# Three PSUM banks for attention scores and two for projections, instead of two and three, in a fused attention and feed-forward kernel

## The chip, the cores and the metric

The kernel runs on one core of one Trainium2 chip. The metric is device time in microseconds, the median of three runs. The kernel before took 746.64 us (746.29 to 746.75).

## What is computed

A transformer block on x of shape (4, 512, 512): layer norm, then attention with 16 heads of 32 and a linear bias, and a gated feed-forward part whose three weight matrices are made from control points by cubic interpolation. Both parts read the same normalized input. Cut to what matters:

```python
xn = _layernorm(x)                                    # 4 batches of 512 rows of 512
q, k, v = (proj(Wq, bq), proj(Wk, bk), proj(Wv, bv))  # xn @ W + bias, 16 heads of 32
scores = einsum('bhqd,bhkd->bhqk', q, k) / sqrt(32) + slope[h] * distance[k]
attn = softmax(where(causal, scores, lowest))
ctx = einsum('bhqk,bhkd->bhqd', attn, v)
attention = ctx @ Wo + bo
gate_w, up_w, down_w = (spline_reconstruct(cp, ...) for cp in (gate_cp, up_cp, down_cp))
ffn = (silu(xn @ gate_w.T) * (xn @ up_w.T)) @ down_w.T
return x + attention + ffn
```

## The kernel before, in words

The program is written out by hand for each engine; semaphores alone tie the engines together, and each engine takes its instructions in the order in which they stand. Attention comes first (up to about 459 us), then the feed-forward part.

**Attention** is a chain of steps, one per head, 16 per batch, over 4 batches without a break between them. TensorE's part is `step` in `attention_tensor`. In step s it makes the scores of head s (`scores`, L689), four query tiles of 128 rows against 256, 256, 384 and 512 keys; it turns the probabilities of head s - 2 (`turn_probs`, L703), and weighs the values of head s - 3 (`weigh_values`, L720 and L723). VectorE adds the bias to a score tile and takes its maximum (`bias_and_max`, L910), copies turned tiles (L919) and normalizes the context (L928 to L936). ScalarE takes exponentials (L1143), rounds the probabilities to 16 bits (L1151) and copies the last turned tile (L1158). GpSimd makes the rest that the rounding leaves (L1256).

**The products between them.** Into the same steps the kernel fits the dense products of this batch and of its neighbours, by the tables `UNITS` and `TURNS`. A product is called by a letter and a number:

- q and k: one of four column chunks of a projection (12 matmuls, L615 to L617); ScalarE reads it twice (L1115, L1124), and the second reading frees its bank.
- v: a row tile of the value projection (12 matmuls); VectorE reads it and frees its bank (`v_take`, L886).
- x: a row tile of the normalized input, turned (4 transposes, L605); ScalarE (L1097) and then VectorE (`x_low`, L878) read it, and VectorE frees its bank.
- c: a chunk of the context, turned (4 transposes, L733); ScalarE (L1164) and then VectorE (`ctx_low`, L943), which frees its bank.
- o: a row tile of the output projection (12 matmuls); VectorE adds the residual (`add_residual`, L950) and frees its bank.
- m: in the last batch, the moments that the feed-forward part needs (L760 to L762; `moment_low`, L1012).

The first product of a step is split: its first six matmuls come between score tiles 1 and 2, three more each behind the turn of probability tile 0 and the weighing of values 2 and 3. The cycle of products repeats for each batch, from step 8 to step 7 of the next batch; `PJ_BODY` lists it.

**The banks.** PSUM has eight: 0, 1 and 6 for these products in turn, 2 and 3 for score tiles, 4 and 5 for turned probabilities, 7 for weighed values. `pj_use` tells which bank a product has and how often it was used before. TensorE waits on `pj_free` of that bank until the reader of the bank's product before is done. For scores it waits on `t_done`: tile i waits until VectorE has read tile i - 2 of the chain of tiles.

```python
def pj_use(key, b):
    times, rest = pj_before(key, b)
    return rest % 3, times * (len(PJ_BODY) // 3) + rest // 3
...
pj_bank, score_bank, av_bank = [psum[0], psum[1], psum[6]], psum[2:4], psum[7]
```

**The end of attention.** Behind the last scores, `attention_tensor` puts nine of twelve matmuls of o0 behind step 17 and of o1 behind step 18 of the last batch (the three that need context chunk 3 are missing), then turns chunk c3, then ends o0 and o1, then does o2 and o3. Meanwhile VectorE also blends weights of the feed-forward part (`taps_op`, L343 and L348), for which SyncE loads 1 MB chunks (`load_factor`, `load_taps`). The feed-forward part begins in banks 2 and 3 and waits for all readers of the other banks before it uses those.

## Time and profile before

| | |
|---|---|
| Median of 3 runs | 746.64 us (746.29 to 746.75) |
| Profiled execution, its own time | 748.68 us |
| Its span, first to last instruction | 746.9 us |
| Granted TensorE clock, mean over the span | 0.975 of full |
| TensorE busy, matmuls | 673.0 us, 90% |
| VectorE busy | 463.3 us, 62% |
| ScalarE busy | 451.8 us, 60% |
| GpSimd busy | 322.3 us, 43% |
| 150 to 250 us (attention, middle): TensorE, VectorE, ScalarE busy | 92.1, 80.9, 81.7 us |
| 500 to 747 us (feed-forward): TensorE, VectorE, ScalarE busy | 237.2, 75.3, 80.9 us |

A row of the order in time gives the start in us from the span's beginning, the duration in us, the engine, the line, the operation, what it writes and reads, the shapes, and how many instructions are merged; in brackets is the engine's idle time before it and who ended that. Rows of TensorE overlap, since matmuls are pipelined: the time from start to start tells their pace, the duration does not. A clock of 1.00 in a row is TensorE's upper level of 2.4 GHz, 0.50 the lower one of 1.2 GHz.

### The profile page before, as it was taken

To read this page: it belongs to the slowest core of one execution; us is meant where nothing else is said; L and a number is where in the kernel's file an instruction comes from. 1 tells how busy PE (TensorE), PEld (TensorE's weight loads), DVE (VectorE), ACT (ScalarE), POOL (GpSimd) and SP (SyncE) were. 2 spreads that over 40 slices of the span, in tenths; PEclk is the share of its full clock that TensorE was granted. 3 is DMA by queue.
4 is the path that set the end of the run, shared out by engine and by line. 5 is a ranking of instruction groups with operands and counts; after the bars stand their busy time and mean duration, and the time that the engine had idled before them with its cause. 6 is when DMAs were issued, how large, how long until landed. Compare 5 with 4: busy or idle time off the path is not lost.

```text
span 746.9 us, 13707 instructions
## 1 busy us (share of the span) xinstructions
PE 673.0 (90%) x4884; PEld 540.0 (72%) x4884; DVE 463.3 (62%) x1287; ACT 451.8 (60%) x717; POOL 322.3 (43%) x188
## 2 busy tenths in 40 slices
PE   4977889989799898899898876888999999999997
PEld 3756678777577776777776665666888888888885
DVE  6477977879877879778799796567441223223212
ACT  5478887877977878878779763444442332332221
POOL 0255554544644545545546430222253236236334
PEclk9988999999999999999999999899999999999999
DMA  9749497476676384863947939874576484244001
GB/s 304 115 71 225 86 259 128 64 135 169 94 204 86 43 140 98 216 86 57 208 76 97 400 97 271 255 220 113 163 245 213 130 244 166 70 143 140 13 1 56
DMA packets 53355, 110.15 MB, mean 147 GB/s; under 512 B 6504, under 2 KB 6760, under 8 KB 51752
## 3 DMA queue, kind: packets, MB, share of 16 engines
q1 hardware_dynamic: 51704, 106.85, 58.6%
q10 hardware_dynamic: 1584, 2.43, 1.3%
q8 instruction: 39, 0.64, 0.4%
q14 instruction: 28, 0.23, 0.1%
HBM read 59.32 MB, written 25.17 MB: 113 GB/s over the span
## 4 chain that ended last, share of the span: by engine, by line
PE 42%; POOL 5%; DVE 4%; issue 4%; ACT 2%; DMA 2%; ACTq 0%; SPq 0%; POOLq 0%; DVEq 0%
PE bank L1601 6%; PE bank L1603 6%; PE bank L1602 6%; PE bank L1588 3%; PE bank L1589 3%; POOL resid L1769 3%; PE bank L615 3%; PE bank L703 3%; PE bank L617 2%; PE bank L616 2%; DMA taps<-windows 2%; PE bank L689 2%; POOL in_lo L1761 1%; PE bank L1576 1%; PE bank L720 1%
## 5 line engine op out<-in xcount | busy, mean ns | idle before, releaser
L1256 POOL TENSOR_TENSOR work<-work 128x1280 f16<-128x1280 f32 x64 | 170.9, 2670 | 174.2 <-ACT work L1151 174.2
L1761 POOL TENSOR_TENSOR in_lo<-inner,in_hi 128x512 fp32r<-128x512 f32 x64 | 83.0, 1299 | 200.0 <-ACT in_hi L1668 200.0
L910 DVE CUSTOM_DVE_ANT_0 work<-bank,dist 128x128 f32<-128x128 f32 (+3 forms) x256 | 115.3, 487 | 59.4 <-PE bank L689 44.9
L1143 ACT ACTIVATE work<-work,neg_max 128x128 f32<-128x128 f32 (+3 forms) x256 | 129.3, 562 | 18.2 <-DVE neg_max L910 18.1
L1718 DVE TENSOR_TENSOR inner<-bank,silu 128x512 f32<-128x512 f32 x64 | 44.1, 688 | 132.3 <-ACT silu L1662 130.7
L1668 ACT CAST in_hi<-inner 128x512 fp32r<-128x512 f32 x64 | 39.7, 620 | 135.2 <-PE bank L1603 134.4
L703 PE MATMUL bank<-ident,work 128*128 128x128 f16 x1280 | 106.0, 226 | 14.6 <-DVE work L919 10.3
L703 PEld LDWEIGHTS bank<-ident,work 128*128 128x128 f16 x1280 | 75.4, 101 | 51.3 <-issue 31.8
L1151 ACT CAST work<-work 128x1280 f16<-128x1280 f32 x64 | 80.6, 1259 | 49.8 <-PE bank L703 48.6
L1601 PE MATMUL bank<-w_room,in_hi 128*128 128x512 f32 x256 | 100.0, 391 | 0.7 <-POOL in_lo L1761 0.7
L1602 PE MATMUL bank<-w_room,in_hi 128*128 128x512 f32 x256 | 99.6, 389 | 0.0
L1603 PE MATMUL bank<-w_room,in_lo 128*128 128x512 f32 x256 | 99.6, 389 | 0.0
L689 PE MATMUL bank<-k_stack,q_stack 96*128 96x256 f32 (+2 forms) x256 | 76.2, 373 | 22.4 <-DVE neg_max L910 18.3
L919 DVE COPY work<-bank 128x256 f16<-128x256 f16 (+2 forms) x192 | 75.6, 418 | 5.8 <-PE bank L703 5.7
L689 PEld LDWEIGHTS bank<-k_stack,q_stack 96*128 96x128 f32 x256 | 45.5, 195 | 38.7 <-DVE neg_max L910 29.6
L720 PE MATMUL bank<-v_parts,work 128*128 128x98 bf16 x640 | 66.7, 211 | 2.0 <-issue 2.0
L1158 ACT COPY work<-bank 128x1024 f16<-128x1024 f16 x64 | 64.4, 1006 | 2.5 <-PE bank L703 2.5
L723 PE MATMUL bank<-v_parts,work 128*128 128x66 bf16 x640 | 64.1, 195 | 0.0
L1588 PE MATMUL bank<-z,wgu_hi 128*128 128x512 f32 x128 | 52.2, 408 | 11.6 <-issue 7.5
L1601 PEld LDWEIGHTS bank<-w_room,in_hi 128*128 128x128 f32 x256 | 48.4, 189 | 12.0 <-POOL in_lo L1761 2.0
L720 PEld LDWEIGHTS bank<-v_parts,work 128*128 128x128 f16 x640 | 52.7, 99 | 5.6 <-issue 2.8
L1602 PEld LDWEIGHTS bank<-w_room,in_hi 128*128 128x128 f32 x256 | 48.1, 188 | 9.9
(113 smaller groups left out, 1313.9 us busy)
## 6 DMA issues: line engine op xcount, KB each, us to landing
q_stack<-parts SPq DMA_DIRECT2D x48, 256.0 KB, 5.8
k_stack<-parts SPq DMA_DIRECT2D x48, 256.0 KB, 6.2
z<-xt_scratch SPq DMA_DIRECT2D x128, 88.0 KB
x_in<-x SPq DMA_DIRECT2D x32, 256.0 KB, 6.7
xt_scratch<-xt_room SPq DMA_DIRECT2D x8, 1024.0 KB, 7.5
xt_room<-xt_scratch SPq DMA_DIRECT2D x6, 1024.0 KB, 10.6
factor<-c_basis SPq DMA_DIRECT2D x5, 1024.0 KB, 11.8
taps<-windows SPq DMA_DIRECT2D x5, 1024.0 KB, 15.8
```

The source lines that it names most:

```text
L689: pe.matmul(score_bank[i % 2][:, 0:n], q_stack[:, at, h, i * P:(i + 1) * P], k_stack[:, at, h, 0:n], start=True, stop=True).then_inc(s_ful ...
L703: mm = pe.transpose(pt_bank[i % 2][:, (part * n + k) * P:(part * n + k + 1) * P], probs16[:, s % 2, part, OFF[i] + k * P:OFF[i] + (k + 1) ...
L720: pe.matmul(bank[:, i * VALUES:(i + 1) * VALUES], probs_t[:, s % 2, at:at + P], v_parts[:, k, s, :], start=(k == 0), stop=False)
L910: dve.tensor_tensor_reduce(probs[:, s % 2, OFF[i]:OFF[i] + n], score_bank[i % 2][:, 0:n], dist[:, S - n:S], -slope(s), 3.4e38, ALU.add, AL ...
L919: dve.tensor_copy(probs_t[:, s % 2, 2 * OFF[i]:2 * OFF[i] + n], pt_bank[i % 2][:, 0:n]).then_inc(pt_free[i % 2], 1)
L1143: e = act.activation(tile, tile, ACT.Exp, bias=neg_max[:, s % 2, i:i + 1], scale=-1.0)
L1151: act.copy(probs16[:, s % 2, 0, :], probs[:, s % 2, :]).then_inc(hi_ready, 1)
L1256: pool.tensor_tensor(probs16[:, s % 2, 1, :], probs[:, s % 2, :], probs16[:, s % 2, 0, :], ALU.subtract).then_inc(lo_ready, 1)
L1601: pe.matmul(sum_bank[i][:, :], hi, wd_hi[:, g, :], start=(g == 0), stop=False)
L1602: pe.matmul(sum_bank[i][:, :], hi, wd_lo[:, g, :], start=False, stop=False)
L1603: mm = pe.matmul(sum_bank[i][:, :], lo, wd_hi[:, g, :], start=False, stop=(g == NG - 1))
L1761: pool.tensor_tensor(in_lo[k % 2][:, :], inner[:, k % 2, :], in_hi[:, k % 2, :].bitcast(F32), ALU.subtract).then_inc(il_ready, 1)
```

## The change

The projection products, turned tiles and moments get two banks, 0 and 1, in turn. The score tiles get three, 2, 3 and 6, in turn over the whole chain of tiles, so that a tile waits until the third tile before it has been read. In the last batch only o0 has nine matmuls put behind step 17; o1 is done whole behind the turn of c3 and the end of o0. `PJ_LAST`, which lists the products of the end in the order of their banks, follows that. At the seam to the feed-forward part the wait that belonged to the third projection bank becomes one for all score tiles.

```diff
@@ -482,7 +482,7 @@
 PJ_BODY_ENDS.insert(PJ_BODY_ENDS.index(("c", 3)) + 1, ("o", 0))
 
 MOMENTS = {12: 0, 13: 1, 14: 2}
-PJ_LAST = [("k", 3), ("c", 1), ("m", 0), ("m", 1), ("m", 2), ("c", 2), ("o", 0), ("o", 1), ("c", 3), ("o", 2), ("o", 3)]
+PJ_LAST = [("k", 3), ("c", 1), ("m", 0), ("m", 1), ("m", 2), ("c", 2), ("o", 0), ("c", 3), ("o", 1), ("o", 2), ("o", 3)]
 PJ_LAST_ENDS = [("k", 3), ("c", 1), ("m", 0), ("m", 1), ("m", 2), ("c", 2), ("c", 3)] + [("o", t) for t in range(QT)]
 
 CARRIED = [("k", 3)] + [("c", c) for c in range(1, KC)] + [("o", t) for t in range(QT)] + [
@@ -501,7 +501,7 @@
 def pj_use(key, b):
 
     times, rest = pj_before(key, b)
-    return rest % 3, times * (len(PJ_BODY) // 3) + rest // 3
+    return rest % 2, times * (len(PJ_BODY) // 2) + rest // 2
 
 
 def pj_total(key, b):
@@ -568,13 +568,13 @@
     at = W_ROOMS * 2 * D
     w_raw = work[:, 0:at].rearrange("p (s c n) -> p s c n", s=W_ROOMS, c=2)
 
-    pj_bank, score_bank, av_bank = [psum[0], psum[1], psum[6]], psum[2:4], psum[7]
+    pj_bank, score_bank, av_bank = psum[0:2], [psum[2], psum[3], psum[6]], psum[7]
     pt_bank = [p[:, :].bitcast(F16) for p in psum[4:6]]
 
     x_ld = sems(ctx, *[f"x_ld{t}" for t in range(QT)])
     w_ld = sems(ctx, *[f"w_ld{n}" for n in range(W_ROOMS)])
     head_ld, = sems(ctx, "first_head_ld")
-    pj_free = sems(ctx, "pj_free0", "pj_free1", "pj_free2")
+    pj_free = sems(ctx, "pj_free0", "pj_free1")
     pt_free = sems(ctx, "pt_free0", "pt_free1")
     stacked = [sems(ctx, f"{m}_stacked0", f"{m}_stacked1") for m in "qk"]
     res_ld = sems(ctx, *[f"res_ld{t}" for t in range(QT)])
@@ -682,11 +682,12 @@
 
                 pe.wait_ge(stacked[0][c % 2], 2 * STACK * b + STACK * (c // 2 + 1))
                 pe.wait_ge(stacked[1][c % 2], 2 * STACK * b + STACK * (c // 2 + 1))
-            if later(b) or 4 * s + i >= 2:
-                pe.wait_ge(t_done, 64 * b + 4 * s + i - 1)
+            use = 64 * b + 4 * s + i
+            if use >= 3:
+                pe.wait_ge(t_done, use - 2)
             n = max(2, i + 1) * P
             at = 1 if not later(b) and s == 0 else c % 2
-            pe.matmul(score_bank[i % 2][:, 0:n], q_stack[:, at, h, i * P:(i + 1) * P],
+            pe.matmul(score_bank[use % 3][:, 0:n], q_stack[:, at, h, i * P:(i + 1) * P],
                       k_stack[:, at, h, 0:n], start=True, stop=True).then_inc(s_full, 1)
 
         def turn_probs(b, s, i):
@@ -830,12 +831,11 @@
             step(B - 1, s, False)
             if s in MOMENTS:
                 moment(MOMENTS[s])
-            if s > H:
-                project_out(B - 1, s - H - 1, (0, 1, 2))
+            if s == H + 1:
+                project_out(B - 1, 0, (0, 1, 2))
         turn_ctx(B - 1, KC - 1)
-        for q in range(2):
-            project_out(B - 1, q, (3,))
-        for q in range(2, QT):
+        project_out(B - 1, 0, (3,))
+        for q in range(1, QT):
             project_out(B - 1, q)
 
     def attention_vector(dve):
@@ -908,7 +908,7 @@
                 dve.wait_ge(s_full, 64 * b + 4 * s + i + 1)
                 dve.nop(nofuse=True)
                 dve.tensor_tensor_reduce(
-                    probs[:, s % 2, OFF[i]:OFF[i] + n], score_bank[i % 2][:, 0:n], dist[:, S - n:S],
+                    probs[:, s % 2, OFF[i]:OFF[i] + n], score_bank[(64 * b + 4 * s + i) % 3][:, 0:n], dist[:, S - n:S],
                     -slope(s), 3.4e38, ALU.add, ALU.min, neg_max[:, s % 2, i:i + 1]).then_inc(t_done, 1)
 
         def take_turned(b, s, i):
@@ -1434,11 +1434,12 @@
         load_taps(sp, 4)
         store_sum(B - 1, QT - 1)
 
-    ended = [0, 0, 0]
+    ended = [0, 0]
     for q in range(QT):
         bank, used = pj_use(("o", q), B - 1)
         ended[bank] = max(ended[bank], used + 1)
-    return (attention_tensor, attention_vector, attention_scalar, attention_gpsimd, attention_sync), (pj_free, ended)
+    return (attention_tensor, attention_vector, attention_scalar, attention_gpsimd, attention_sync), (
+        pj_free + [t_done], ended + [4 * H * B])
 
 
 BATCHES = [B - 1, *range(B - 1)]
```

Where the change moves things, the order of TensorE's instructions shows it. The first place is the beginning of step 8 of batch 1 (of each batch alike): the last values weighed before k3, k3's first six matmuls (L615 to L617), then score tiles 2 and 3. The names are banks by number, and in brackets stand the semaphores waited for. Before:

```order
L720 MATMUL bank7<-v_parts,work 128x98
L723 MATMUL bank7<-v_parts,work 128x66
L615 MATMUL bank1<-xt_room,w_room 128x512 [waits pj_free1]
L616 MATMUL bank1<-xt_room,w_room 128x512
L617 MATMUL bank1<-xt_room,w_room 128x512
...
L689 MATMUL bank2<-k_stack,q_stack 128x384 [waits t_done]
L689 MATMUL bank3<-k_stack,q_stack 128x512 [waits t_done]
L703 MATMUL bank4<-ident16,work 128x128 [waits pt_free0,p_lo_ready,p_hi_ready]
```

And with the change:

```order
L721 MATMUL bank7<-v_parts,work 128x98
L724 MATMUL bank7<-v_parts,work 128x66
L615 MATMUL bank0<-xt_room,w_room 128x512 [waits pj_free0]
L616 MATMUL bank0<-xt_room,w_room 128x512
L617 MATMUL bank0<-xt_room,w_room 128x512
...
L690 MATMUL bank6<-k_stack,q_stack 128x384 [waits t_done]
L690 MATMUL bank2<-k_stack,q_stack 128x512 [waits t_done]
L704 MATMUL bank4<-ident16,work 128x128 [waits pt_free0,p_lo_ready,p_hi_ready]
```

No instruction has moved; k3 waits for another bank, the one that q3 of step 7 was written to instead of o3's, and score tile 2 has bank 6 to itself where it shared bank 2 with tile 0.

The second place is the end of attention on TensorE, behind the last values weighed. Before, o1's nine matmuls (bank 6, of which the last group is shown), the turn of c3, and the ends of o0 and o1:

```order
L615 MATMUL bank6<-w_room,ctx_t 128x512
L616 MATMUL bank6<-w_room,ctx_t 128x512
L617 MATMUL bank6<-w_room,ctx_t 128x512
L733 MATMUL bank0<-ident,ctx_sb 128x128 [waits ctx_ready,pj_free0]
L733 MATMUL bank0<-ident,ctx_sb 128x128 x3
L615 MATMUL bank1<-w_room,ctx_t 128x512 [waits pj_free0]
L616 MATMUL bank1<-w_room,ctx_t 128x512
L617 MATMUL bank1<-w_room,ctx_t 128x512
L615 MATMUL bank6<-w_room,ctx_t 128x512
```

And with the change:

```order
L734 MATMUL bank1<-ident,ctx_sb 128x128 [waits ctx_ready,pj_free1]
L734 MATMUL bank1<-ident,ctx_sb 128x128 x3
L615 MATMUL bank0<-w_room,ctx_t 128x512 [waits pj_free1]
L616 MATMUL bank0<-w_room,ctx_t 128x512
L617 MATMUL bank0<-w_room,ctx_t 128x512
L615 MATMUL bank0<-w_room,ctx_t 128x512 [waits pj_free0]
```

The turn of c3 now stands nine matmuls further ahead, and o1 (from the last row shown) comes whole behind o0 and in o0's bank, for whose reader it waits.

## Rows read from the trace of the kernel before

**Rows 1.** Idle time of TensorE by group of instructions: busy and mean ns | idle before, releaser.

```profile
L689 PE MATMUL bank<-k_stack,q_stack 96*128 96x384 f32 x64 | 25.2, 393 | 19.1 <-DVE neg_max L910 18.3
```

**Rows 2.** Order in time, step 8 of batch 1: k3, q3's reader, score tile 2.

```profile
183.96 0.48 PE L615 MATMUL bank<-xt_room,w_room 128*128 128x512 f32 x1
...
186.03 0.78 ACT L1124 ACTIVATE parts<-bank,b_scaled,q_scale 128x512 fp32r<-128x512 f32 x1
...
186.47 0.84 PE L689 MATMUL bank<-k_stack,q_stack 96*128 96x384 f32 x2 [0.88 <-DVE neg_max L910]
```

**Rows 3.** Order in time, step 9: x0 and x1, k3's reader, score tile 2.

```profile
190.59 0.68 DVE L943 TENSOR_TENSOR ctx_t<-bank,ctx_t 128x512 fp32r<-128x512 f32 x1
...
190.89 1.10 PE L605 MATMUL bank<-ident,x_in 128*128 128x128 f32 x8
...
193.27 0.69 ACT L1124 ACTIVATE parts<-bank,b_qk 128x512 fp32r<-128x512 f32 x1
...
193.36 0.84 PE L689 MATMUL bank<-k_stack,q_stack 96*128 96x384 f32 x2 [1.37 <-DVE neg_max L910]
...
195.04 1.34 DVE L869 SCALAR_TENSOR_TENSOR shift<-meanvar,rstd 128x2 f32<-128x2 f32 x1
...
196.65 0.96 PE L703 MATMUL bank<-ident,work 128*128 128x128 f16 x14 [1.58 <-DVE work L919]
```

**Rows 4.** Order in time, steps 10 and 11: x3, v0 and the readers of x0 to x3.

```profile
200.06 0.40 PE L703 MATMUL bank<-ident,work 128*128 128x128 f16 x4 [0.56 <-ACT work L1158]
...
202.35 1.27 DVE L878 TENSOR_TENSOR xt_room<-bank,xt_room 128x512 fp32r<-128x512 f32 x2
...
203.08 0.66 PE L605 MATMUL bank<-ident,x_in 128*128 128x128 f32 x4 [0.89 <-DVE xt_room L878]
...
204.06 0.48 PE L615 MATMUL bank<-w_room,xt_room 128*128 128x512 f32 x1
...
205.51 1.29 DVE L878 TENSOR_TENSOR xt_room<-bank,xt_room 128x512 fp32r<-128x512 f32 x2 [0.88 <-ACT xt_room L1097]
```

**Rows 5.** Order in time, step 12: k0 and q0's reader.

```profile
212.86 0.77 ACT L1124 ACTIVATE parts<-bank,b_scaled,q_scale 128x512 fp32r<-128x512 f32 x1
...
212.88 0.48 PE L615 MATMUL bank<-xt_room,w_room 128*128 128x512 f32 x1
```

**Rows 6.** Order in time, steps 13, 14 and 3: v1, v2, k2, and readers before them.

```profile
218.19 0.68 DVE L943 TENSOR_TENSOR ctx_t<-bank,ctx_t 128x512 fp32r<-128x512 f32 x1
...
218.48 0.48 PE L615 MATMUL bank<-w_room,xt_room 128*128 128x512 f32 x1
...
226.86 0.48 PE L615 MATMUL bank<-w_room,xt_room 128*128 128x512 f32 x1
...
227.36 0.69 DVE L886 TENSOR_TENSOR v_room<-bank,bv_all 128x512 f32<-128x512 f32 x1
...
260.81 0.40 PE L615 MATMUL bank<-xt_room,w_room 128*128 128x512 f32 x1
...
261.01 0.69 DVE L950 TENSOR_TENSOR x_in<-bank,x_in 128x512 f32<-128x512 f32 x1
...
261.50 0.40 PE L615 MATMUL bank<-xt_room,w_room 128*128 128x512 f32 x1
```

**Rows 7.** Order in time on VectorE, last batch, steps 9 and 12.

```profile
399.63 0.56 DVE L910 CUSTOM_DVE_ANT_0 work<-bank,dist 128x384 f32<-128x384 f32 x1 [0.30 <-PE bank L689]
...
419.65 1.37 DVE L343 TENSOR_TENSOR taps<-taps,factor 128x512 f32<-128x512 f32 x1 [2.44 <-DMA taps<-windows]
```

**Rows 8.** Order in time, end of attention and early feed-forward part.

```profile
450.92 0.50 PE L615 MATMUL bank<-w_room,ctx_t 128*128 128x512 f32 x1 [1.76 <-DVE ctx_t L943]
...
451.92 0.69 DVE L950 TENSOR_TENSOR x_in<-bank,x_in 128x512 f32<-128x512 f32 x1 [0.46 <-PE bank L617]
...
481.88 0.87 DVE L343 TENSOR_TENSOR taps<-taps,factor 128x512 f32<-128x512 f32 x1 [2.23 <-DMA taps<-windows]
```

**Rows 9.** Sums of a stretch: length, busy PE, PEld, DVE, ACT, POOL, granted clock, DMA share, GB/s.

```profile
299.50:302.80 3.30, 3.30 (x24) 2.93 (x24) 2.23 (x9) 2.83 (x4) 1.15 (x2) 0.50 0.40 83
```

## The prediction

> **What bounds the kernel now.** I read the table of busy times first (TensorE 90% of the span), then the idle time of TensorE by group of instructions, then the order in time on each engine, always with one question: when did an engine finish with a bank, and when did TensorE start on the next product in the same bank? Attention runs as a chain of steps, one per head. A step that carries one or two products is bound by TensorE and lasts 5.6 us (k0 to v1) or 8.8 us (v0 to k0) by the starts in [rows 4 to 6]. A step without one is shorter, and there VectorE hardly rests. The target of the change is plain in [rows 1]: score tile 2 of a head (384 columns) waits in all 19.1 us for VectorE to have read tile 0, and nothing comparable stands before another matmul. That looks like a prize, but most of it lies in steps without a product. In a cycle of 16 steps in the middle of the run only step 8 (0.88 us, [rows 2]), step 9 (1.37 us, [rows 3]) and, shorter, step 10 have such a wait.
>
> The third projection bank is what the profile must be asked about. With three banks a product waits for the reader of the third product before it, with two for the reader of the second. I call the products q, k, v, x (turned input), c (turned context) and o as the kernel does. Their order in a cycle is k3 | x0 x1 | x2 x3 | v0 q0 c1 | k0 | v1 q1 | v2 | v3 c2 | k1 | q2 | o0 c3 | k2 | o1 | o2 | o3 | q3 c0, from step 8 on. TensorE takes its instructions in order, so a wait holds everything behind it: the scores of the same step, the turns of probabilities, the weighing of values. From the release to the start of the waiting matmul the trace has 0.05 to 0.08 us (c0's reader ends at 190.59 + 0.68 = 191.27, and x1, the second half of the eight transposes from 190.89, cannot start before; x3 waits 0.89 us for x0's reader, the first half of the pair at 202.35; [rows 3, 4]). I use 0.05.
>
> **The change part by part, two banks for the products.** Each place is: end of the new reader, plus 0.05, less today's start.
>
> Step 8, k3 behind q3. ScalarE ends with q3 at 186.03 + 0.78 = 186.81; k3 starts at 183.96 [rows 2]. Wait: 2.90. Its six matmuls are followed by score tile 2, which today starts at 186.47 after waiting; a matmul of 512 columns comes every 0.23 (three from 260.81 to 261.50, [rows 6]), so six take some 1.4, with the start 1.46, and the tile now goes at 186.86 + 1.46 = 188.32. TensorE is 1.85 later, and the removed score wait is already counted in that.
>
> Step 9, x1 behind k3. x0 now follows c0's reader as x1 does today, and VectorE there is 1.75 late; that costs little. But x1 needs ScalarE to be done with k3, today at 193.27 + 0.69 = 193.96 [rows 3]. ScalarE is some 1.75 later, since its exponentials follow the delayed tiles, so x1 starts at about 195.77 instead of 191.36. Four transposes later (0.48) comes score tile 2, at 196.25 instead of 193.36: 2.9 late. Part of it comes back at the turn that stands idle 1.58 us for VectorE today (196.65). VectorE's own delay there is between 1.8 and 2.9: its 128x2 instruction at 195.04 takes 1.34 us, which is waiting and not work, and what it shares with GpSimd is only about 1.8 late. I take 1.8, and keep 2.9 for the range.
>
> Step 10. The turn at 200.06 waits for ScalarE [rows 4], whose exponentials of step 9 depend on the late tiles; I get 2.25. Then x2 needs x0's reader and x3 needs x1's, the second of the pair that ends at 202.35 + 1.27 = 203.62. So x3 starts at 203.62 + 2.25 + 0.05 = 205.92 instead of 203.08: 2.85 late.
>
> Step 11, v0 behind x2. The pair of readers at 205.51 lasts 1.29, so x2's ends near 206.16, and it hangs on ScalarE (0.88 idle, [rows 4]), hence on the 2.25: 208.45 instead of 204.06. From here TensorE is **4.4 us late**.
>
> In the steps after that every reader is itself led by TensorE in its step, so nothing is absorbed and the waits add up. k0 behind q0: 212.86 + 0.77 + 0.05 - 212.88 = 0.80 [rows 5]. v1 behind c1: 218.19 + 0.68 + 0.05 - 218.48 = 0.44. v2 behind v1: 227.36 + 0.69 + 0.05 - 226.86 = 1.24. k2 behind o0, its immediate forerunner in the same step: 261.01 + 0.69 + 0.05 - 260.81 = 0.94 [rows 6]. Two more places repeat a pattern: k1 behind v3 as v2 behind v1 (1.24), q2 behind c2 as v1 behind c1 (0.44). Sum 5.1. All other products find their bank free well before they start, and I cost them at nothing: their cover is the rest of a step's matmuls between them and the reader, and without it each would add what its reader is late.
>
> So a cycle costs 4.4 + 5.1 = 9.5, and there are three: **28.5**. Bounds: 1.8 + 5.1 = 6.9 a cycle if steps 9 to 11 give back all but VectorE's delay, 10.6 if the 1.34 us stays; 20.7 to 31.8 in all.
>
> The last batch has k3 behind q3 once more, with no score wait beside it: **+2.9**. VectorE's slack in steps 9 to 12 does not win it back, because at 419.65 VectorE waits for the DMA of the second weight chunk [rows 7], and that DMA is issued only once k3 has been read. Bounds 1.9 and 3.2.
>
> **Three banks for the scores.** What it still gives lies where VectorE sets the pace. There its third tile stands 0.30 us for a matmul that was issued only after tile 0 was read [rows 7]; the row stands for four steps in succession. Steps 1 and 4 to 7 of batch 0 show the same, some 0.3 each: **-1.4** (0 to -2.5, the first because the clock is low there and TensorE may bind). In the last batch steps 9 to 11 gain nothing for the DMA wait just named, steps 13 to 15 some **-0.8** (0 to -2).
>
> **The end.** Nine matmuls of o1 move from before the turn of c3 to after it: 9 x 0.23 = 2.05. In addition o1 now shares its bank with o0 and waits for its reader: o0's last three are issued from 450.92, its reader ends at 451.92 + 0.69 = 452.61, so about 1.0. But VectorE stands 2.23 us at 481.88 for a weight DMA [rows 8], which hangs on the queue of SyncE and not on these products, and the feed-forward part starts slowly anyway. I take **+0.3** (0 to +3). The moved matmuls bring nothing forward: c3's reader on ScalarE is busy with weights until then, and today's 1.76 us of idle time at 450.92 stays.
>
> **Sum.** 28.5 + 2.9 - 1.4 - 0.8 + 0.3 = 29.5. The profiled execution took 748.68 us, 2.04 more than the median of 746.64. 748.68 + 29.5 - 2.04 gives **776.1 us**. Differences within 0.2% (1.5 us) count as none, as a measurement of this kernel can't tell them apart.
>
> **Rivals.** *The readers catch up* (0.14). Steps 8 to 11 give most of it back: with scores out earlier, ScalarE reaches k3 and x2 sooner. For it: three of the idle gaps of [rows 2 to 4] lie here. Against it: q3's reader, the first in the chain, depends on nothing that the change speeds up. Then 18 to 21 us more, 766.
>
> *The clock falls* (0.15). In one cycle of three the granted clock is at half from 299.5 to 302.8, TensorE busy all the time [rows 9], after the gaps of its steps 8 to 10; the other two cycles have the same gaps at full clock. Longer gaps could make that the rule. A stretch of 3.3 us at half costs at most 1.65 us of TensorE's work; two in each of three cycles and two more give 8 x 1.65 = 13 at most, some 8 likely as part falls into waits: 784. The Trainium skill, TensorE: Matmul & The Clock Gate, "A second HAM failure mode: psum-queue depth-cycling", tells of a kernel whose small idle times between groups, as it went round its PSUM banks, made the clock swing; by that this case would come out. The same page, "Loop structure matters more than you think", has it that copying a result out of PSUM does not cool the array; the two undisturbed cycles here agree with that.
>
> *Faster* (0.02). The wait of tile 2 is what delays VectorE and ScalarE, and once it is gone they release each bank before TensorE comes for it. It decides if q3's reader ends before 183.9, 2.9 us sooner than in [rows 2]. Then all 19.1 us of [rows 1] are the prize at most, 727.5; by VectorE's 0.30 us [rows 7] in each of some 16 steps it is 5 us, 741.8.
>
> *Nothing happens* (0.01), the waits on two banks are met anyway: 746.6.
>
> The forecast itself has 0.68, with 771 to 781 as its own range. The range 765 to 786 takes in the bounds of the cycles and most of the rivals next to it. Faster 0.02, same 0.01, slower 0.97.
>
> **What would show it.** In the profile after: score tile 2's idle time falls from 19.1 to under 3 us. In its place TensorE stands before L615 and L605 for readers (L1124, L878, L886, L943, L950), some 30 us in all, k3's four times about 2.9. The time from one cycle's x0 to the next one's grows by about 9.5. Within the cycle, v0 starts 4.4 later against step 7. The feed-forward part, from 490 on, keeps its length. I am wrong if a cycle grows by under 7 us, or if the score waits stay, or if the clock is at half in more than six stretches of the attention part.

## The result, and the profile after

| | before | after |
|---|---|---|
| Median of 4 runs each, side by side | 746.46 us (744.31 to 746.75) | 783.18 us (781.11 to 784.38) |
| Ratio to before, 95% interval | | 1.0495 (1.047 to 1.0521) |
| Profiled execution, its own time | 748.68 us | 784.38 us |
| Its span | 746.9 us | 782.6 us |
| Granted TensorE clock, mean over the span | 0.975 | 0.963 |
| TensorE busy, matmuls | 673.0 us, 90% | 683.2 us, 87% |

Slower by 36.7 us. The forecast was 776.1 with a range of 765 to 786: the sign and the range held, the size was 7.1 us short. All times here are medians; one execution of a later kernel (hybrid), which took 946.13 us at a mean clock of 0.657, is left out.

The head of the page after. VectorE and ScalarE do the same work as before (463.3 and 451.8 us there); TensorE has 10 us more of busy time for the same 4884 matmuls, which is the first hint that its clock and not only its waits changed:

```profile
span 782.6 us, 13708 instructions
...
PE 683.2 (87%) x4884; PEld 546.4 (70%) x4884; DVE 460.0 (59%) x1287; ACT 452.5 (58%) x717; POOL 322.2 (41%) x188
...
PEclk9999889999899999899999999899999999999999
```

To see where the time went I cut both traces at the same matmul, the first score tile of step 8, with the end of attention for a last cut. Busy time by stretch, before (columns: from and to, length, busy PE, PEld, DVE, ACT, POOL with instruction counts, granted clock, DMA share, GB/s):

```profile
183.40:286.27 102.87, 94.98 (x932) 75.65 (x930) 83.45 (x277) 84.59 (x133) 53.80 (x26) 1.00 0.61 114
286.27:391.46 105.19, 97.53 (x931) 76.91 (x930) 85.17 (x280) 85.34 (x133) 54.70 (x26) 0.98 0.63 124
391.46:459.00 67.54, 54.75 (x552) 44.52 (x550) 56.46 (x163) 46.74 (x69) 26.95 (x11) 0.95 0.69 201
459.00:746.90 287.90, 269.13 (x1149) 218.61 (x1147) 99.74 (x142) 99.26 (x175) 102.85 (x80) 0.98 0.50 150
```

The same view after:

```profile
195.68:312.07 116.39, 100.53 (x932) 79.22 (x930) 82.37 (x277) 85.02 (x133) 53.69 (x26) 0.96 0.55 101
312.07:428.98 116.91, 100.98 (x932) 79.20 (x929) 83.58 (x280) 85.65 (x133) 54.57 (x26) 0.96 0.56 111
428.98:498.00 69.02, 51.41 (x529) 41.78 (x528) 52.64 (x156) 46.80 (x69) 26.91 (x11) 0.90 0.67 199
498.00:782.60 284.60, 268.94 (x1172) 218.65 (x1170) 104.73 (x149) 99.04 (x175) 102.92 (x80) 1.00 0.50 151
```

The first cycle shown grows by 13.5 us (forecast 9.5), the second by 11.7, where the kernel before itself had lost time at half clock [rows 9]. Of the 13.5, 5.55 are more busy time of TensorE for the same 932 matmuls, at a mean clock of 0.96 instead of 1.00. The cycle ahead of them grew by 14.6: TensorE was 2.3 ahead of the kernel before at the first score tile of step 8 of batch 0 and 12.3 behind at that of batch 1. The end of attention and the feed-forward part gave back 3.3.

TensorE's waits after (what waited, for whom, us in total, times, the longest):

```profile
PE bank L615 <- ACT parts L1124: 12.9, 7, 2.7
PE bank L690 <- DVE neg_max L910: 9.5, 7, 2.5
...
PE bank L615 <- DVE v_room L886: 6.5, 6, 1.1
PE bank L605 <- ACT parts L1124: 6.1, 3, 2.0
...
PE bank L615 <- DVE xt_room L878: 4.3, 3, 1.4
PE bank L615 <- DVE ctx_t L943: 4.2, 7, 2.6
...
PE bank L605 <- DVE xt_room L878: 4.0, 3, 1.3
```

Apart from the rows of L690, these are the product banks' readers that the forecast named, in its places. The first row is k3 behind q3, four times 2.7, and three times k0 behind q0. The score waits did not vanish. Groups by shape, after, against [rows 1]:

```profile
L690 PE MATMUL bank<-k_stack,q_stack 96*128 96x512 f32 x64 | 28.9, 452 | 9.7 <-DVE neg_max L910 9.5
...
L690 PE MATMUL bank<-k_stack,q_stack 96*128 96x384 f32 x64 | 25.4, 396 | 0.0
```

Tile 2 (384 columns) no longer waits for tile 0. But tile 3 (512 columns) now does, for what is tile 0 three tiles back: half of the 19.1 us moved one matmul on. None of its 9.7 us stands in the three cycles; its waits are in steps 1 to 6 of batch 0 and 9 to 15 of the last batch, where VectorE sets the pace.

Last, the order in time at the three places of a cycle where TensorE stands longest (start, duration, what, idle before it in brackets), k3 in step 8, x1 in step 9, v0 in step 11:

```profile
199.15 0.79 PE L615 MATMUL bank<-xt_room,w_room 128*128 128x512 f32 x1 [2.75 <-ACT parts L1124]
199.74 0.63 PE L616 MATMUL bank<-xt_room,w_room 128*128 128x512 f32 x1
200.16 0.63 PE L617 MATMUL bank<-xt_room,w_room 128*128 128x512 f32 x1
...
201.87 0.91 PE L690 MATMUL bank<-k_stack,q_stack 96*128 96x384 f32 x2
...
209.47 1.11 PE L605 MATMUL bank<-ident,x_in 128*128 128x128 f32 x4 [2.02 <-ACT parts L1124]
...
222.93 0.69 PE L615 MATMUL bank<-w_room,xt_room 128*128 128x512 f32 x1 [1.44 <-DVE xt_room L878]
...
225.55 0.95 PE L690 MATMUL bank<-k_stack,q_stack 96*128 96x384 f32 x2
```

Behind the wait, k3's matmuls come every 0.42 us, where [rows 6] has 0.23, and score tile 2 starts 2.72 us after k3 instead of 1.46. Those stretches in the view by window (columns as above):

```profile
199.20:202.60 3.40, 3.40 (x8) 2.43 (x8) 0.06 (x1) 1.07 (x3) 3.01 (x2) 0.50 0.00 0
209.40:212.80 3.40, 3.33 (x26) 2.88 (x26) 1.75 (x5) 1.85 (x5) 3.40 (x2) 0.50 0.00 0
223.10:226.50 3.40, 3.40 (x11) 2.41 (x11) 0.66 (x2) 0.24 (x1) 0.34 (x1) 0.50 0.71 261
```

The granted clock is 0.50, the level of 1.2 GHz, and each stretch begins as TensorE resumes behind one of the three waits. It is the same in the next cycle (315.2, 325.5 and 339.1, 3.4 us each) and in batch 0 (83.1, 93.4 and 103.6). The one exception is the last k3: it waits 2.75 us at 432.4, and the clock stays at 1.00 until 444.9. Half clock adds up to 58.0 us of the span after and 37.9 of the span before.

### The profile page after: what moved, and what is told of

Same layout as the page of the kernel before. It is cut to its first block, busy times and chain, and to the rows that moved or that the text cites. A ratio compares the mean times of both kernels' runs of the same rounds, so it can differ in the third digit from the quotient of the medians.

```text
span 782.6 us, 13708 instructions
## 1 busy us (share of the span) xinstructions
PE 683.2 (87%) x4884; PEld 546.4 (70%) x4884; DVE 460.0 (59%) x1287; ACT 452.5 (58%) x717; POOL 322.2 (41%) x188
## 4 chain that ended last, share of the span: by engine, by line
PE 63%; DVE 9%; issue 7%; ACT 7%; DMA 5%; POOL 4%; SPq 4%; ACTq 0%; POOLq 0%; DVEq 0%
PE bank L615 8%; PE bank L704 7%; PE bank L617 6%; PE bank L616 6%; PE bank L1602 6%; PE bank L1604 6%; PE bank L1603 6%; PE bank L690 4%; DMA taps<-windows 4%; PE bank L1589 3%; PE bank L1590 3%; POOL resid L1770 3%; PE bank L721 2%; ACT work L1158 2%; SPq L330 2%
## 5 line engine op out<-in xcount | busy, mean ns | idle before, releaser
L1762 POOL TENSOR_TENSOR in_lo<-inner,in_hi 128x512 fp32r<-128x512 f32 x64 | 83.1, 1301 | 196.5 <-ACT in_hi L1669 196.5
L704 PE MATMUL bank<-ident,work 128*128 128x128 f16 x1280 | 108.5, 228 | 12.7 <-ACT work L1158 6.5
L690 PE MATMUL bank<-k_stack,q_stack 96*128 96x256 f32 (+2 forms) x256 | 76.1, 372 | 14.2 <-DVE neg_max L910 9.5
L919 DVE COPY work<-bank 128x256 f16<-128x256 f16 (+2 forms) x192 | 76.0, 418 | 11.3 <-PE bank L704 11.2
L615 PE MATMUL bank<-xt_room,w_room 128*128 128x512 f32 x120 | 54.6, 455 | 19.3 <-ACT parts L1124 12.9
L721 PE MATMUL bank<-v_parts,work 128*128 128x98 bf16 x640 | 68.3, 213 | 2.0 <-issue 2.0
L690 PEld LDWEIGHTS bank<-k_stack,q_stack 96*128 96x128 f32 x256 | 46.6, 202 | 24.8 <-DVE neg_max L910 13.8
L1589 PE MATMUL bank<-z,wgu_hi 128*128 128x512 f32 x128 | 50.4, 394 | 7.9 <-DVE inner L1719 5.1
L1602 PEld LDWEIGHTS bank<-w_room,in_hi 128*128 128x128 f32 x256 | 48.0, 188 | 11.9 <-POOL in_lo L1762 2.0
```

Source lines behind the costliest of these rows:

```text
L615: pe.matmul(bank[:, :], l_hi, r_hi, start=(k == 0), stop=False)
L690: pe.matmul(score_bank[use % 3][:, 0:n], q_stack[:, at, h, i * P:(i + 1) * P], k_stack[:, at, h, 0:n], start=True, stop=True).then_inc(s_f ...
L704: mm = pe.transpose(pt_bank[i % 2][:, (part * n + k) * P:(part * n + k + 1) * P], probs16[:, s % 2, part, OFF[i] + k * P:OFF[i] + (k + 1) ...
L721: pe.matmul(bank[:, i * VALUES:(i + 1) * VALUES], probs_t[:, s % 2, at:at + P], v_parts[:, k, s, :], start=(k == 0), stop=False)
L1602: pe.matmul(sum_bank[i][:, :], hi, wd_hi[:, g, :], start=(g == 0), stop=False)
L1762: pool.tensor_tensor(in_lo[k % 2][:, :], inner[:, k % 2, :], in_hi[:, k % 2, :].bitcast(F32), ALU.subtract).then_inc(il_ready, 1)
```

## The experiments

Eleven runs of ten kernels follow, in three groups, each group beside the kernel before on a chip of its own. The theory after the first look was: the bank waits cost what the forecast says (9.5 a cycle), and the rest is the clock, which falls behind k3, x1 and v0. The rival: the rest is more waiting, and the clock is only seen where it does no harm. To read them all I take one measure, how much later than in the kernel before the first score tile of a step starts, in us (batch.step):

| | before starts | after | fill | two_early | two_late | k3_only | k3_filled |
|---|---|---|---|---|---|---|---|
| 0.8 | 80.54 | -2.3 | -1.2 | -0.8 | -1.3 | -1.2 | -0.6 |
| 0.12 | 109.48 | 6.2 | 3.1 | 3.6 | -0.9 | 4.4 | 2.2 |
| 1.8 | 183.40 | 12.3 | 8.4 | 3.5 | 4.5 | 4.5 | 2.2 |
| 1.12 | 212.33 | 20.5 | 13.1 | 9.5 | 4.5 | 7.7 | 5.1 |
| 2.8 | 286.27 | 25.8 | 18.4 | 9.5 | 10.0 | 7.7 | 5.1 |
| 2.12 | 315.76 | 33.2 | 22.1 | 17.5 | 10.7 | 10.2 | 7.4 |
| 3.8 | 391.46 | 37.5 | 26.4 | 17.5 | 16.9 | 10.1 | 7.4 |
| 3.12 | 412.12 | 40.3 | 28.1 | 21.8 | 16.7 | 14.5 | 10.5 |
| span | 746.9 | +35.7 | +23.3 | +17.6 | +14.0 | +10.5 | +2.8 |

The columns are single traces and carry their own scatter: at 0.8, three kernels that change nothing ahead of that point (end_only, two_late, hybrid_last) start between 1.3 us earlier and 0.6 later than before.

### end_only: the new end with the old banks

In the kernel before, `PJ_LAST` and the end of `attention_tensor` as in the change, nothing else:

```diff
-            if s > H:
-                project_out(B - 1, s - H - 1, (0, 1, 2))
+            if s == H + 1:
+                project_out(B - 1, 0, (0, 1, 2))
```

> The kernel before with only the end of the change: o1 whole behind the turn of c3, three product banks and two score banks as before. First theory (the prediction's): the nine moved matmuls are hidden, so 0 to +3 us, likely +0.3 (746 to 750). Rival: the profile after loses 3.4 us less over the seam to the feed-forward part than before attention's end (its delay is 39.1 us at c2 and 35.7 us at the end of the span), and if the moved matmuls are what gains that, this kernel is 2 to 4 us faster than before.

Measured: 746.39 us (744.13 to 747.93, 10 runs) against 746.58, ratio 0.9984 (0.9962 to 1.0005). The moved matmuls cost nothing that can be measured. They belong to the change by need, not by choice: with the old end and two banks, the early parts of o0 and o1 would hold both banks, c3 would wait for o0's reader, and o0 for c3. That is read from the order; no kernel with it ran.

### two_and_two: the changed kernel without the third score bank

```diff
-    pj_bank, score_bank, av_bank = psum[0:2], [psum[2], psum[3], psum[6]], psum[7]
+    pj_bank, score_bank, av_bank = psum[0:2], psum[2:4], psum[7]
-            if use >= 3:
-                pe.wait_ge(t_done, use - 2)
+            if use >= 2:
+                pe.wait_ge(t_done, use - 1)
```

> The changed kernel with two banks for scores again, so bank 6 is unused: the cost of the lost product bank without the gain of the third score bank. First theory: the score bank gained 1.4 + 0.8 us in the stretches where VectorE sets the pace and some 1.1 us in step 8 of each cycle is regained whether by one or the other, so this one is 2 to 5 us slower than the changed kernel (785 to 788). Rival: the third score bank gains far more inside the cycles (all of its 19.1 us, 9.6 of which are left): 792 or more.

Measured: 789.0 us (786.35 to 795.99, 4 runs), ratio 1.0583 (1.0513 to 1.0653). So the product bank that is lost costs 42 us, and the third score bank gives back some 4 to 6 (789.0 against 783.18; 4.0 by the two spans). The intervals of the two ratios overlap a little (from 1.0513, up to 1.0521), so the size of that gain is loose; 789.0 is just above what was expected (785 to 788). Groups by shape of this kernel:

```profile
L690 PE MATMUL bank<-k_stack,q_stack 96*128 96x512 f32 x64 | 28.9, 452 | 0.0
L690 PE MATMUL bank<-k_stack,q_stack 96*128 96x384 f32 x64 | 26.1, 408 | 11.9 <-DVE neg_max L910 11.0
```

Tile 2 waits 11.9 us here and not 19.1: the bank waits alone take 7 us of the score waits over, as the forecast said of steps 8 to 10. The third score bank then turns 11.9 into 9.7 on tile 3.

### fill: useless matmuls in the waits

The changed kernel; ahead of k3, x1 and v0 TensorE multiplies old data into the score bank that comes next, 12, 8 and 6 matmuls, and scores overwrite them. The waits stay in place; TensorE is only kept busy in them.

```diff
+        def keep_busy(b, s, n):
+            use = 64 * b + 4 * s + 2
+            pe.wait_ge(t_done, use - 2)
+            for _ in range(n):
+                pe.matmul(score_bank[use % 3][:, :], w_hi[:, 1, 0, 0:P], w_hi[:, 1, 0, :], start=True, stop=True)
...
+            if s == 8:
+                keep_busy(b, s, 12)
+            if s == 11 and carry:
+                keep_busy(b, s, 6)
...
+                    if key[1] == 1:
+                        keep_busy(b, s, 8)
```

> The changed kernel, with matmuls of no use put into TensorE's waits: 12 ahead of k3 in step 8, 8 ahead of x1 in step 9, 6 ahead of v0 in step 11, written to the bank of the next score tile, which overwrites them. They replace idle time by busy time and take away no wait. Clock theory: the three waits of each cycle are what lowers the granted clock (it is 0.50 for 3.4 us behind each of them in the profile after), which costs some 4 us a cycle on top of the waits; then the clock stays at full there, the cycle falls from 116 us to about 112.5 and the time to 770 to 775. Rival: the low clock only goes along with the waits and the extra 4 us a cycle are longer ways through ScalarE and VectorE; then nothing changes, or the 26 matmuls add up to 1 us a cycle: 783 to 786.

Measured: 771.48 us (769.2 to 771.96, 4 runs), ratio 1.0321 (1.0286 to 1.0355). With 90 matmuls more the kernel is 11.7 us faster than the changed one, as the clock theory expected (770 to 775) and the rival did not (783 to 786). The mean granted clock of the four runs is 0.984, that of the changed kernel's four 0.966. k3 and v0 in its trace, the order in time:

```profile
192.38 2.99 PE L779 MATMUL bank<-w_room 128*128 128x512 f32 x12
195.30 0.50 PE L615 MATMUL bank<-xt_room,w_room 128*128 128x512 f32 x1
...
196.78 0.58 PE L690 MATMUL bank<-k_stack,q_stack 96*128 96x384 f32 x2
...
217.18 0.40 PE L615 MATMUL bank<-w_room,xt_room 128*128 128x512 f32 x1
...
218.58 0.57 PE L690 MATMUL bank<-k_stack,q_stack 96*128 96x384 f32 x2
```

and by window the cycle, from the first score tile of step 8 to the next one, and the stretches behind k3 and v0:

```profile
191.83:304.66 112.83, 103.00 (x957) 81.60 (x956) 81.61 (x277) 84.97 (x133) 53.80 (x26) 0.98 0.55 104
...
195.40:198.80 3.40, 3.40 (x30) 2.61 (x31) 1.53 (x7) 1.94 (x5) 2.99 (x2) 1.00 0.00 0
216.20:219.60 3.40, 3.40 (x17) 2.58 (x17) 1.92 (x7) 1.27 (x4) 1.40 (x1) 1.00 0.77 280
```

k3 to score tile 2 takes 1.48 us and v0 to score tile 2 1.40, where the changed kernel needs 2.72 and 2.62. The cycle is 9.96 us longer than before, against a forecast of 9.5, and by the table above steps 8 to 11 cost 4.6 (forecast 4.4) and the rest 5.3 (forecast 5.1). In the changed kernel the same rows read 8.2 and 5.3. The whole difference lies in steps 8 to 11, and it is the clock. Not all of it was removed: this cycle of fill still has 3.4 us of half clock at 210.6, between x1 and v0, as TensorE resumes behind a wait of 1.31 us for ScalarE. The other two cycles have none in these steps, and there steps 8 to 11 cost 4.3 and 3.7.

### two_early and two_late: two banks for one part of the cycle

The kernel before with three banks in general; two_early gives two banks only to q3, c0, k3, x0 to x3 and v0 of each cycle and to the last k3, two_late only to q0 to k2. Each use takes the bank longest out of use among those allowed:

```diff
+PJ_BANKS = in_turn(PJ_USES, lambda n: (0, 1) if 14 <= n <= 88 and (n - 16) % 24 in (22, 23, 0, 1, 2, 3, 4, 5) else (0, 1, 2))
```

(two_late has `16 <= n < 88 and 6 <= (n - 16) % 24 <= 18`.)

> The kernel before with the products in two banks only from q3 of step 7 to v0 of step 11 of each cycle (and for k3 of the last batch), three banks elsewhere, two for the scores. The waits are those on k3, x0 to x3 and v0. The prediction priced them at 4.4 us a cycle and 2.9 us at the end, 16 in all: 763. With the clock theory (0.50 for 3.4 us behind k3, x1 and v0) each cycle loses some 4 us more: 27 in all, 774. In the two-and-two kernel the waits of the whole cycle cost 42.4 us; the two parts should sum to that.

> The kernel before with the products in two banks only from q0 of step 11 to k2 of step 3 of each cycle. The waits are those on k0, v1, v2, k1, q2 and k2, none above 1.3 us. Both theories expect 5.1 to 5.4 us a cycle, 15.3 to 16.2 in all and a clock as before: 762 to 763. Rival: waits this short are absorbed, or they too lower the clock: below 755 or above 767.

Measured: two_early 769.66 us (766.26 to 772.88, 4 runs), ratio 1.0314 (1.0273 to 1.0355), 22.7 more than before; two_late 762.66 us (761.48 to 764.56, 4 runs), ratio 1.0208 (1.0178 to 1.0239), 15.7 more. The late part is what the forecast's terms give (3 x 5.1 = 15.3), with waits of 0.3 to 1.1 us. The early part is not: the terms give 3 x 4.4 + 2.9 = 16.1, and it is 6.6 over. The clock theory had put it at 27, so it lies between the two expectations. By the table it costs 4.4, 6.0 and 8.0 in the three cycles, with half clock at 92.5, at 191.5 and 201.8, and at 300.7 and 311.0 with 321.2. That this is the clock fits the runs too: their mean granted clock is 0.962 in two_early, 0.972 in two_late and 0.973 in the kernel before beside them. So waits of 0.3 to 1.1 us left the mean clock as it was. The two parts together make 38.4, two_and_two 42.4 with an interval of 38 to 49.

### k3_only and k3_filled: one wait, empty and filled

k3_only makes k3 alone wait for q3's reader, as in the change, once a batch. k3_filled puts 12 useless matmuls into the same wait, into the free bank 6:

```diff
+PJ_BANKS = in_turn(PJ_USES, lambda n: (0, 1) if 14 <= n <= 88 and (n - 16) % 24 in (22, 23, 0) else (0, 1, 2))
...
+            if s == 8:
+                pe.wait_ge(pj_free[2], PJ_BANKS[:24 * b + 16].count(2))
+                for _ in range(12):
+                    pe.matmul(pj_bank[2][:, :], w_hi[:, 1, 0, 0:P], w_hi[:, 1, 0, :], start=True, stop=True)
```

> The kernel before with one more wait a cycle: q3 and c0 are put into the banks so that k3 has to wait for q3's reader (2.9 us four times), all other products as before. If only the wait counts, TensorE is 1.85 us later behind score tile 2, that stays 1.8 through step 9, and the last one costs 2.9: +8.3, 755. With the clock theory the half clock behind the wait adds 1.4 us each: +13, 760.

> The same as the one-wait kernel, with twelve matmuls of no use in the wait (2.7 us, into bank 6, which is free there). Wait and order are the same, only the array is busy instead of idle. Clock theory: the difference to the one-wait kernel is what the clock costs, 4 to 6 us for four waits: about 755. Rival (the array's idle time has nothing to do with the clock): no difference.

Measured: k3_only 759.34 us (756.19 to 760.19, 4 runs), ratio 1.0154 (1.012 to 1.0188); k3_filled 751.34 us (750.98 to 753.99, 6 runs), ratio 1.0062 (1.0041 to 1.0083). Four waits cost 12.4 us empty, as the clock theory expected (13), and 4.4 filled, which is 4 us less than even that theory gave (about 755). k3_only, the order in time at the second k3:

```profile
191.37 0.79 PE L629 MATMUL bank<-xt_room,w_room 128*128 128x512 f32 x1 [2.74 <-ACT parts L1138]
191.96 0.63 PE L630 MATMUL bank<-xt_room,w_room 128*128 128x512 f32 x1
...
194.09 0.87 PE L703 MATMUL bank<-k_stack,q_stack 96*128 96x384 f32 x2
```

k3_filled, the same:

```profile
186.16 3.00 PE L803 MATMUL bank<-w_room 128*128 128x512 f32 x12
189.08 0.50 PE L629 MATMUL bank<-xt_room,w_room 128*128 128x512 f32 x1
189.42 0.40 PE L630 MATMUL bank<-xt_room,w_room 128*128 128x512 f32 x1
...
190.57 0.57 PE L703 MATMUL bank<-k_stack,q_stack 96*128 96x384 f32 x2
```

2.72 us from k3 to score tile 2 at half clock, 1.49 at full; the forecast had 1.46. The 8 us between the kernels are not four times this 1.2, though. By the table the filled kernel saves 2.8 us in steps 8 to 11 of batch 0, 0.3 and 0.2 in the next two batches, and 1.2 in the last; less the 0.6 by which it is behind at the start, that makes 3.9 by step 12 of the last batch (14.5 against 10.5). In batch 1 most of the saving is there at the last score tile of step 8 (3.1 us grown against 1.7) and gone at step 12 (3.2 against 2.8). What takes it is the clock, which falls later instead. k3_filled runs 6.8 us at half clock from 199.6 on, behind TensorE's wait for VectorE in step 9; k3_only has the same wait and goes on at full clock. The wait and the same 6.8 us of the program, k3_only first and k3_filled second:

```profile
204.30 0.96 PE L717 MATMUL bank<-ident,work 128*128 128x128 f16 x14 [1.59 <-DVE work L933]
203.40:210.20 6.80, 4.60 (x62) 3.70 (x62) 6.32 (x22) 6.24 (x11) 4.47 (x3) 1.00 0.60 88
```

```profile
200.47 1.67 PE L717 MATMUL bank<-ident,work 128*128 128x128 f16 x14 [1.59 <-DVE work L937]
199.60:206.40 6.80, 5.82 (x50) 5.06 (x51) 5.17 (x19) 5.77 (x10) 4.44 (x3) 0.50 0.60 89
```

It is the same in batch 2 (6.8 us from 305.4 on), and it is the place where the kernel before falls in its third cycle [rows 9]. So filling one wait moved the half clock and did not remove it: 48.3 us of half clock in the span against 50.6. Over all runs the mean granted clock is 0.972 filled and 0.966 empty.

The rest of the 8 us lies in the last batch, where another 3.6 appear in step 13. VectorE's waits for the weight chunks differ, k3_only first and k3_filled second:

```profile
DVE taps L343 <- DMA taps<-windows: 2.1, 1, 2.1
```

```profile
DVE taps L343 <- DMA taps<-windows: 0.4, 1, 0.4
```

The two loads of taps are issued behind the DMA of k3 (420.3 and 421.3 us in k3_only, 416.0 and 417.0 in k3_filled), and in k3_filled they land almost in time, so that TensorE, which stands 2.70 us for VectorE in k3_only at 435.7 and has half clock behind it, does not stand. That is one profiled execution of each; whether the rest of the 8 us is always got this way stays open.

### hybrid and its halves: the third bank where no product needs it

The first group's traces showed where the third score bank gives something: where VectorE sets the pace. There a product bank is idle. So hybrid is the kernel before with a third bank for scores only in steps 3 to 6 of batch 0 and from step 9 of the last batch; the product banks are three elsewhere, and the end is the old one.

```diff
+PJ_BANKS = in_turn(PJ_USES, lambda n: (0, 1) if PJ_LAST_K3 < n < PJ_LAST_O0 else (0, 1, 2))
+SCORE_BANKS = in_turn(4 * H * B, lambda u: (0, 1, 2) if 12 <= u < 4 * (HALF - 1) or u >= 4 * H * (B - 1) + 36 else (0, 1))
...
+            bank, read, taken = score_use(b, s, i)
+            if read:
+                pe.wait_ge(t_done, read)
+            if taken:
+                n_before = PJ_FIRST_Q3 if not later(b) else PJ_LAST_K3 + 1
+                pe.wait_ge(pj_free[2], PJ_BANKS[:n_before].count(2))
```

> The kernel before with the third score bank only where the products don't need theirs: steps 3 to 6 of batch 0, and from step 9 of the last batch to its last score tile; elsewhere the banks and the end are as before. The prediction priced the third score bank at 1.4 us early and 0.8 us late. Theory: 0.5 to 2.5 us faster than before (744 to 746). Rival: what VectorE gains there is lost again to the product steps and to the DMA wait behind step 12: no difference (746.5).

Measured: 742.53 us (740.68 to 745.5, 9 runs), ratio 0.9949 (0.9925 to 0.9973), a little more gain than expected (744 to 746). A gain this small asked for a second look, with its halves: hybrid_first has only the `12 <= u < 4 * (HALF - 1)` part of the condition, hybrid_last only the other.

> The kernel of run hybrid once more, beside its two halves on one chip. If the 4 us of the first time belong to the kernel: 741 to 744 against 746.6. If they came from how that chip happened to run: within 0.2% of the kernel before. The profile cannot decide it: in the run before, TensorE stood only 2.2 us ahead at the end of attention, and the rest of the span's gain lay in the stretch from 450 to 510, where end_only had the same gain and the same median as the kernel before.

> Only the first half of hybrid: the third bank goes to the scores in steps 3 to 6 of batch 0, everything else as before. In the profile of hybrid TensorE was 1.1 us ahead from step 8 of batch 0 on, of which the run end_only, which changes nothing there, had 0.7. Theory that the bank gives what VectorE's pace gives: -0.4 to -1.4, so 745.5 +- 0.7. Rival, that the gain of hybrid lies in the last batch alone: 746.6.

> Only the second half of hybrid: the third bank goes to the scores from step 9 of the last batch to the end of attention, where no product but c1, the moments and c2 needs one. In the profile of hybrid the last batch gained between 0.2 (step 15, tile 3) and 1.2 us (step 12). Theory: -0.5 to -2, so 745.3 +- 0.8; c1 and the moments, which have two banks there, wait for nothing new. Rival, that the seam after attention also profits, since TensorE comes to it with the clock up: -3 to -4.

Measured against 746.38 us (17 runs): hybrid_again 742.73 us (740.71 to 745.99, 7 runs), ratio 0.9947 (0.9928 to 0.9966); hybrid_first 743.32 us (740.38 to 743.91, 6 runs), ratio 0.995 (0.9931 to 0.9968); hybrid_last 744.43 us (740.77 to 745.22, 11 runs), ratio 0.9963 (0.9947 to 0.998). So the gain belongs to the kernel: 3.7 us faster than the kernel before, 40 faster than the changed one. Each half is worth 2 to 3 us; together they give less than their sum, within the intervals. Groups by shape of hybrid_again show that it isn't the idle time that goes:

```profile
L719 PE MATMUL bank<-k_stack,q_stack 96*128 96x512 f32 x64 | 28.7, 448 | 8.2 <-DVE neg_max L942 8.2
L719 PE MATMUL bank<-k_stack,q_stack 96*128 96x384 f32 x64 | 24.6, 384 | 11.4 <-DVE neg_max L942 11.1
```

8.2 + 11.4 is as much as the 19.1 of before: TensorE runs a tile further ahead and then waits there. One thing that is gained is clock: the mean granted clock of the runs is 0.981 in hybrid_again and 0.982 in hybrid_first, against 0.975 in the kernel before beside them. hybrid_first comes out beyond both of its expectations (745.5 and 746.6); its clock alone could account for that, since 0.007 of 745 us is an estimated 5 us of work, more than the 3.1 gained. In hybrid_last the clock is that of before (0.976); there the gain would be the little time in which VectorE stands for a tile issued late [rows 7], which is argued, not shown. No run separates the two.

## Why the prediction was right, and where it was short

- **Two banks for the products cost TensorE waits at k3, x1, x3, v0 and six later places: right.** k3 waits 2.74 to 2.75 us (forecast 2.90), its releaser is L1124. The 5.1 us of the later steps came out as 5.3 in the cycle shown.
- **Steps 8 to 11 cost 4.4 us: the step that was mis-sized.** They cost 8.5, 8.2 and 7.4 in the three cycles, 24.1 where the forecast has 13.2. The working took a matmul of 512 columns at 0.23 us everywhere, that is, full clock. With the waits filled the same steps cost 4.3, 4.6 and 3.7, so the chain of readers was right, and what was missing is the clock term: some 3.6 us in the cycle shown, about 1.2 behind each of k3 and v0 (2.72 against 1.48 us, 2.62 against 1.40) and the rest around x1.
- **The rival "the clock falls" was therefore no rival but a term.** Its 8 us and 784 were nearly the result (783.18; fill against after: 11.7 us). I gave it 0.15 because two of three cycles of before had idle gaps at full clock. Those gaps were at most 1.4 to 1.6 us long [rows 3]; the forecast itself put 2.9 us of idle time in one piece, and twice more soon after, into every cycle, and [rows 9] already showed half clock behind such a gap. The Trainium skill, TensorE: Matmul & The Clock Gate, "A second HAM failure mode: psum-queue depth-cycling", has idle times between groups of matmuls that go round the PSUM banks swing the clock. The trace agrees in part: the clock fell behind bank waits of 2.75, 2.0 and 1.4 us, while the shorter ones of two_late, at most 1.1 us, left it at 0.972 against 0.973. In the same page, "Loop structure matters more than you think", the copy out of PSUM does not cool the array if the next matmuls follow immediately; here they did not (k3 stood 2.75 us), and the two statements do not conflict.
- **The third score bank: -1.4 and -0.8.** TensorE was 2.3 us ahead when the first k3 came, of which kernels that change nothing there show up to 1.3, so the -1.4 is neither shown nor refuted. In the last batch it went from 40.4 behind at k3 to 39.2 at the last score tile, so -1.2. In steps 4 to 7 of the last batch it gained another 1.0 (38.5 to 37.5), which two_and_two does not have, and which the working had not looked for.
- **Last k3 +2.9: right** (37.5 to 40.4).
- **The end +0.3: within what can be measured nothing** (end_only). Yet the trace shows -3.5 from the last score tile to the last instruction. This is the profiled execution of before: it has 13.6 us of half clock between 463 and 491, the one after 6.8. end_only gains as much there (span 743.0) at an unchanged median, so that is most likely no effect of the change.
- **What would show it.** Tile 2's idle time fell under 3 us, to 0.0, but I had not seen that outside the cycles the wait can go to tile 3 (9.7). TensorE's waits for the five readers are 42 us (the rows above without the score's, 3.1 for L950, and 0.8 more of L605 for L943) and not some 30. "I am wrong if the clock is at half in more than six stretches of the attention part": there are fifteen up to 498 us, and the kernel before has five up to 459. The test was set rightly, and it says that the mechanism was incomplete.

The sum, with what was measured: -2.3 (start) + 39.8 (three cycles) + 2.9 (k3) - 1.2 (last batch) - 3.5 (end) = 35.7, the difference of the spans. The three cycles alone are 11.3 us above their 28.5 and outside their bounds (20.7 to 31.8). That the time still fell into 765 to 786 is in part luck: the start, the last batch and the end came out 5.1 us better than their terms, by amounts that single traces can't settle, and the range was wide enough for a rival that turned out to be a term.

## What to carry to other kernels

Before a buffer is moved from one ring to another, read for each ring how late its reader is at every use: a wait that VectorE's pace sets only moves on to the next tile when a buffer is added, while a ring that was just deep enough turns every use into a wait. If a forecast puts idle time of 2 to 3 us in one piece before dense matmuls, price those matmuls at half clock too (here 1.2 us behind k3 and behind v0), and test it by filling the wait with useless matmuls. Fill all the long waits of a stretch and read the clock over the whole of it: with one wait filled, the half clock came at a later one. A bank can also be lent: to the scores only in the steps in which no product needs it, which beat both kernels.

## What I had not expected of the hardware

- A wait costs more than its length, and useless work can pay: 90 useless matmuls made the changed kernel 11.7 us faster (783.18 to 771.48). Twelve in each of four waits made k3_only 8 us faster (759.34 to 751.34), of which 3.6 lie in one step of the last batch.
- The same kernel does not have its half-clock stretches in the same places each time. In batch 0, hybrid was profiled with half clock from 39.5 for 10.2 us and from 66.8 for 3.4, hybrid_again from 44.1 for 3.4 us alone; at step 8 the one is 1.1 us ahead of before, the other 3.1. A difference of 2 us between two single traces is no effect of an edit here.
